# Three stages of a graph network kernel re-ordered: maxima scanned a block ahead, tables split by two engines, and some one-hot halves built by ScalarE

## The reference

```python
Q = relu(x @ query_kernel + query_bias)[row]        # 8 heads of 16
K = relu(x @ key_kernel + key_bias)[col]
V = (x @ kernel)[col]
att = sum(Qh * Kh, axis=-1)                          # scores, one per edge and head
smax = segment_max(att, row); sexp = exp(att - smax[row])
alpha = sexp / segment_sum(sexp, row)[row]
out = segment_sum(Vh * alpha, row) + bias
x = layernorm(x + out)        # then L1 (edge MLP with batch norms), L2 (graph convolution), L3 (GIN with MLP)
```

## Time and profile before

| | us |
|---|---|
| median of 3 runs | 11621.56 (11620.08 to 11631.48) |
| the profiled execution, its own time | 11608.96 |
| its span in the profile | 11607.3 |
| DVE busy in the span | 8568.2 (74%) |
| PE busy in the span | 8888.0 (77%) |
| ACT busy in the span | 4243.8 (37%) |

### The profile page before, as it was taken

How to read it: one execution, slowest core, us unless ns; L and a number is a source line. 1 busy time by engine, 2 the same in 40 slices (tenths; PEclk the granted TensorE clock), 3 DMA queues, 4 the chain that set the end, 5 groups by cost and what they waited for, 6 DMA issues and landing times. The chain is left out here.

```text
span 11607.3 us, 329950 instructions
## 1 busy us (share of the span) xinstructions
PE 8888.0 (77%) x100902; PEld 7202.7 (62%) x101099; DVE 8568.2 (74%) x17497; ACT 4243.8 (37%) x8562; POOL 1651.7 (14%) x2115
## 2 busy tenths in 40 slices
PE   6144557885888744799994888799899959949996
PEld 5132224664777644799994666433899946649995
DVE  7497777777999856666666666666788877788887
ACT  0020001111333211455552333477677736613332
POOL 0010000110000000466661000000000003301110
PEclk5555555555999855899997999899999979979997
DMA  1100000000444311233331999687455510000000
GB/s 37 13 0 11 4 4 8 11 11 21 162 160 162 125 33 32 96 122 124 123 124 67 328 324 327 234 251 250 129 144 144 144 41 5 5 3 3 3 3 12
DMA packets 616505, 1103.16 MB, mean 95 GB/s; under 512 B 119451, under 2 KB 207094, under 8 KB 616443
## 3 DMA queue, kind: packets, MB, share of 16 engines
q1 hardware_dynamic: 486939, 922.77, 25.0%
q10 hardware_dynamic: 121152, 168.86, 3.9%
q0 software_dynamic: 8352, 10.85, 0.4%
HBM read 901.13 MB, written 201.10 MB: 95 GB/s over the span
## 5 line engine op out<-in xcount | busy, mean ns | idle before, releaser
L2364 POOL TENSOR_TENSOR acc<-acc,m_sum 128x544 f32<-128x544 f32 (+1 forms) x637 | 809.8, 1271 | 1289.7 <-ACT m_sum L2331 1012.8
L2294 PE MATMUL m_sps<-m_msg,m_oh 128*128 128x136 f32 x5096 | 722.8, 286 | 0.0
L2229 DVE TENSOR_TENSOR m_msg<-m_vps,m_msg 128x512 f32<-128x512 f32 x637 | 440.5, 692 | 367.0 <-PE m_vps L2270 292.2
L2684 PE MATMUL u_sps<-u_r,u_oh 128*128 128x128 f32 x5096 | 677.8, 276 | 28.7 <-ACT u_r L2642 28.7
L2483 DVE BATCH_NORM_STATS2 stats<-t_es 128x512 f32 x637 | 442.3, 694 | 331.0 <-ACT t_es L2516 329.3
L2668 PE MATMUL u_zps<-fcs,u_a 128*128 128x128 f32 x5112 | 676.9, 276 | 6.9 <-ACT u_a L2636 6.9
L1983 ACT COPY s_qs<-s_qps 128x512 f32<-128x512 f32 x637 | 372.9, 585 | 800.9 <-PE s_qps L1964 727.8
L1397 PE MATMUL sp_out_x<-x,sp_adj_x 128*128 128x128 f32 x4802 | 661.9, 281 | 0.0
L1964 PE MATMUL s_qps<-q_parts,s_oht 128*128 128x128 bf16 x7203 | 511.5, 220 | 194.0 <-DVE s_oht L1461 168.2
L2569 PE MATMUL g_z<-g_a,fcT 128*128 128x512 f32 x1274 | 611.5, 615 | 62.9 <-ACT g_a L2558 52.8
L1381 PE MATMUL sp_aps_x<-sp_ohw_x,sp_oh_x 128*128 128x128 bf16 x7644 | 545.8, 219 | 144.7 <-DVE sp_ohw_x L1348 144.7
(11 more groups left out here) (582 smaller groups left out, 21327.1 us busy)
## 6 DMA issues: line engine op xcount, KB each, us to landing
u_e<-e_tiles SPq DMA_DIRECT2D x640, 256.0 KB, 2.8
e_tiles<-t_es ACTq DMA_DIRECT2D x637, 256.0 KB, 5.3
g_e<-e_tiles SPq DMA_DIRECT2D x637, 256.0 KB, 3.4
s_rows<-bucket_rows SPq DMA_DIRECT2D x148, 768.0 KB, 4.1
m_rows<-bucket_rows SPq DMA_DIRECT2D x148, 768.0 KB, 4.1
t_rows<-bucket_rows SPq DMA_DIRECT2D x148, 768.0 KB, 6.8
s_rows<-bucket_rows SPq DMA_DIRECT2D x49, 1024.0 KB, 5.3
m_rows<-bucket_rows SPq DMA_DIRECT2D x49, 1024.0 KB, 5.3
```

Source lines behind the costliest of these rows:

```text
L2294: last = nc.tensor.matmul(sps[x][:, at:at + M], oh[x][:, j * P:(j + 1) * P], msg[x][:, j * M:(j + 1) * M], start=True, stop=True)
L2364: nc.gpsimd.tensor_tensor(at, at, sums[x][:, 0:n * M], ALU.add).then_inc(added, 1)
L2684: last = nc.tensor.matmul(sps[:, :], oh[x][:, j * P:(j + 1) * P], zr[x][:, j * D:(j + 1) * D], start=(q == 0 and j == 0), stop=(q == last_ ...
```

## The change

Three edits.

1. `phase_parts`: the table is cut into two halves `u` of 25 blocks. DVE keeps the four half subtractions and two half casts; ACT does the other four half casts. Four more semaphores are taken.
2. `phase_scores`: for the sets 3, 5, 7, 9 and 11 (`shared`) DVE builds only the left 512 columns. ACT builds the right 512 by two instructions: the square of (row number - node number), and then relu(1 - that), which is 1 where they are equal and else 0. The square stands ahead of ACT's copy of set `q = p - 2`, the relu behind it. PE waits for ACT's half too, and DVE, before it frees a piece, waits for ACT's sets of that piece.
3. `phase_maxima`: the turning of `x_att` and the scan of window `w + 1` are issued within window `w`. Window 0's stand ahead of the loop, and SP loads one window more behind its loop. The three block numbers of the spare tiles are packed into one integer, so that one register load and shifts take the place of three register loads.

```diff
+    def overs(self, eng, s, b):
+        packed = eng.value_load(self.ovpk[0:1, bass.ds(b, 1)], min_val=0, max_val=64 ** self.OV - 1)
+        return [((packed >> 6 * j) & 63).with_bounds(min_val=0, max_val=s.NB) for j in range(self.OV)]
...
@@ phase_parts
+        at = [slice(0, s.NB1 // 2), slice(s.NB1 // 2, s.NB1)]
+        def cast(copy, u, c):
+            return copy(p4[:, at[u], c, :], blocks(rest if c else src)[:, at[u], :]).then_inc(made[u], 1)
             @block.vector
-                c.step(nc.vector.tensor_copy(p4[:, :, 0, :], blocks(src)))
-                c.step(nc.vector.tensor_tensor(blocks(rest), blocks(src), p4[:, :, 0, :], ALU.subtract))
-                c.step(nc.vector.tensor_copy(p4[:, :, 1, :], blocks(rest)))
-                c.step(nc.vector.tensor_tensor(blocks(rest), blocks(rest), p4[:, :, 1, :], ALU.subtract))
-                c.step(nc.vector.tensor_copy(p4[:, :, 2, :], blocks(rest)))
+                def lessen(u, c):
+                    dve.wait_ge(made[u], c + 1)
+                    nc.vector.tensor_tensor(blocks(rest)[:, at[u], :], blocks(rest if c else src)[:, at[u], :], p4[:, at[u], c, :],
+                                            ALU.subtract).then_inc(less[u], 1)
+                cast(nc.vector.tensor_copy, 0, 0)
+                lessen(0, 0)
+                lessen(1, 0)
+                lessen(0, 1)
+                lessen(1, 1)
+                dve.wait_ge(less[1], 2)
+                cast(nc.vector.tensor_copy, 1, 2)
...
+            @block.scalar
+                cast(nc.scalar.copy, 1, 0)
+                for u, c in ((0, 1), (1, 1), (0, 2)):
+                    act.wait_ge(less[u], c)
+                    cast(nc.scalar.copy, u, c)
...
@@ phase_scores
+        shared = range(3, NQ - 1, 2)
...
-                    row_hots(nc, k, B, oht[r], buf[n], q).then_inc(oht_made[r], 1)
+                    if q in shared:
+                        nc.vector.tensor_scalar(oht[r][:, 0:GE], row_of(0, q), k["iota1_p"][:, 0:1], None, ALU.is_equal).then_inc(oht_made[r], 1)
+                    else:
+                        row_hots(nc, k, B, oht[r], buf[n], q).then_inc(oht_made[r], 1)
                     if q + 1 == B.pieces[n][1]:
                         dve.wait_ge(oht_made[r], O.before(w, q) + 1)
+                        here = [p for p in shared if p < B.pieces[n][1]]
+                        if here:
+                            dve.wait_ge(act_made, w * len(shared) + (len(here) + 1))
                         dve.sem_inc(rows_free[n], 1)
...
                     for q in range(NQ):
                         x = X.slot(q)
+                        p, n = q + 2, w * len(shared)
+                        if p in shared:
+                            back, user = O.user_before(p)
+                            act.wait_ge(rows_in[piece_of(B, p)], w * 16 + 16)
+                            act.wait_ge(k_made[X.slot(user)], X.before(w, user) + (1 + k0 + back * X.uses[X.slot(user)]))
+                            act.wait_ge(act_made, n + (shared.index(p) + 1))
+                            nc.scalar.activation(far[:, :], row_of(1, p), ACT.Square, bias=minus[:, 0:1]).then_inc(far_made, 1)
                         act.wait_ge(q_made[x], X.before(w, q) + 1)
                         act.wait_ge(prod_made[x], X.before(w, q) + 1)
                         nc.scalar.copy(qs[x][:, :], qps[x][:, :]).then_inc(q_copied[x], 1)
+                        if p in shared:
+                            act.wait_ge(far_made, n + shared.index(p) + 1)
+                            nc.scalar.activation(oht[O.slot(p)][:, GE:], far[:, :], ACT.Relu, bias=1.0, scale=-1.0).then_inc(act_made, 1)
...
@@ phase_maxima, vector
-                    dve.wait_ge(turned, w + 2)
-                    dve.wait_ge(back, w + 1)
-                    nc.vector.tensor_tensor_scan(run[:, :], mask[:, bass.ds(half * GE, GE)], tps[0:HQ, :], 0.0, ALU.mult, ALU.max).then_inc(scanned, 1)
                     hot(0)
                     hot(1)
                     b = B.block(dve, s, w)
-                    vs = [dve.value_load(B.ovsb[0:1, bass.ds(b * OV + j, 1)], min_val=0, max_val=s.NB) for j in range(OV)]
+                    vs = B.overs(dve, s, b)
                     hot(2)
                     hot(3)
                     dve.wait_ge(split, w * 5 + 2)
                     nc.vector.tensor_tensor(rest[:, :], bps[:, :], parts[0][:, :], ALU.subtract).then_inc(split, 1)
+                    scan(w + 1)
                     dve.wait_ge(split, w * 5 + 4)
                     nc.vector.tensor_tensor(rest[:, :], rest[:, :], parts[1][:, :], ALU.subtract).then_inc(split, 1)
```

More of the change, by code:

```diff
@@ L1094, in _ @@
                 c.go(nc.vector.tensor_copy(B.ovsb[:, :].rearrange("p (b q) -> p b q", q=OV), v4[0:1, :, F:]))
+                c.step(nc.vector.tensor_copy(pk[:, :], v4[0:1, :, F + OV - 1]))
+                for q in range(OV - 2, -1, -1):
+                    c.step(nc.vector.tensor_scalar(pk[:, :], pk[:, :], 64.0, None, ALU.mult))
+                    c.step(nc.vector.tensor_tensor(pk[:, :], pk[:, :], v4[0:1, :, F + q], ALU.add))
+                c.go(nc.vector.tensor_copy(B.ovpk[:, :], pk[:, :]))
                 c.step(nc.vector.tensor_copy(xc[:, :], xk))
@@ L1741, in phase_parts @@
         step, stored = sem("parts_step"), sem("parts_stored")
+        made, less = ([sem(f"parts_{x}{u}") for u in range(2)] for x in ("made", "less"))
         p4 = parts[:, :].rearrange("p (b c f) -> p b c f", c=3, f=D)
+        at = [slice(0, s.NB1 // 2), slice(s.NB1 // 2, s.NB1)]
+        def cast(copy, u, c):
+            return copy(p4[:, at[u], c, :], blocks(rest if c else src)[:, at[u], :]).then_inc(made[u], 1)
         with nc.Block() as block:
@@ L2006, in _, with load @@
             def _(sp):
-                with sp.Fori(0, B.windows(sp, s)) as w:
-                    half = w & 1
-                    sp.wait_ge(turned, w + 1)
-                    sp.wait_ge(free, w + 1)
+                nw = B.windows(sp, s)
+                def load(n, w):
+                    half = n & 1
+                    sp.wait_ge(turned, n + 1)
+                    sp.wait_ge(free, n + 1)
                     sp.sem_inc(go, 1)
@@ L2017, in _ @@
                                  ).then_inc(ins, 16)
-                    sp.wait_ge(ins, w * 32 + 32)
+                    sp.wait_ge(ins, n * 32 + 32)
                     sp.sem_inc(go, 1)
+                with sp.Fori(0, nw) as w:
+                    load(w, w)
+                load(nw, 0)
+                sp.wait_ge(att_in, nw * 32 + 32)
+                sp.sem_inc(go, 1)
             @block.tensor
@@ L2025, in _, with turn @@
                 pe.sem_inc(split, 1)
-                with pe.Fori(0, B.windows(pe, s)) as w:
+                def turn(w):
                     pe.wait_ge(att_in, w * 32 + 32)
@@ L2031, in _ @@
                     last.then_inc(turned, 1)
+                turn(0)
+                with pe.Fori(0, B.windows(pe, s)) as w:
                     pe.wait_ge(scanned, w + 2)
@@ L2036, in _ @@
                     last.then_inc(back, 1)
+                    turn(w + 1)
                     pe.wait_ge(split, w * 5 + 6)
@@ L2056, in _, with scan @@
                 r_last, S = R.slot(NQ - 1), s.NB * H
+                def scan(w):
+                    half = w & 1
+                    dve.wait_ge(ins, w * 32 + 32)
+                    dve.wait_ge(turned, w + 2)
+                    dve.wait_ge(back, w + 1)
+                    nc.vector.tensor_tensor_scan(run[:, :], mask[:, half * GE:(half + 1) * GE] if isinstance(w, int) else mask[:, bass.ds(half * GE, GE)],
+                                                 tps[0:HQ, :], 0.0, ALU.mult, ALU.max).then_inc(scanned, 1)
+                scan(0)
                 with dve.Fori(0, B.windows(dve, s)) as w:
                     half = w & 1
-                    dve.wait_ge(ins, w * 32 + 32)
                     def hot(q):
```

20 lines of the change are left out of this document (17 added, 3 removed).

## The result

| | before | after |
|---|---|---|
| median, us | 11620.93 (4 runs, 11620.08 to 11631.48) | 11549.77 (4 runs, 11540.65 to 11562.99) |
| ratio | | 0.9938, 95% interval 0.9926 to 0.9951 |
| the profiled execution's own time, us | 11608.96 | 11562.99 |

The change makes the kernel 71 us faster. The forecast was 104 us faster (11517); 11550 lies inside its range of 11485 to 11555, 33 us above its middle.

A forecast was written before the change was run, and what follows sets the result against it. No engine bounds the whole kernel; stages run one behind another, each edit acting on its own. 37 + 24 + 43 = 104 us off 11621.6 gives about 11517 us, 8 in 10 within 11485 to 11555.

The forecast's parts named there:

- Splits: forecast 37: Splits: six calls save 6.25 us each, ACT's casts being covered by DVE's work; 37 us, bounds 33 and 41.
- 2 x 3.49/2: Splits: DVE's two half casts take half of 3.49 us each, part of 17.15 us a call.
- The bound of 33: Splits: the lower bound of the gain, 33 us, with each handover costing 0.3.
- Scores: forecast 24: Scores: half one-hots save 0.60 us a window, less queue instructions; net 0.48, 24 us in 49 windows, bounds 0 and 46.
- 3 x 0.08 = 0.24 if all is exposed, and about half of it if the queue prepared it: Scores: cost per window, in us, of one queue instruction more for DVE at each of three piece ends.
- rival (b): Scores give nothing, because ACT's square pushes the copy or a half's pitch equals the whole's: 11541 us; chance 13%.
- rival (d): Scores: ACT reloads its function table between copy, square and relu, losing 314 us: slower, 11830 us; chance 2%.
- Maxima: forecast 43: Maxima: the cycle falls from 13.12 to 12.25 us, 0.87 less in 49 windows; 43 us, bounds 28 and 60.
- H + 5.9: Maxima: DVE's own route reaches the scan 5.9 us after H, the end of a window's one-hots.
- H + 6.0: Maxima: SP's mask load lets the scan start 6.0 us after the end of a window's one-hots, as late as DVE.
- rival (a): Maxima: the mask decides, taking over 5 us from issue to use; cycle 13.1, no gain there, 11560 us; chance 9%.
- rival (c): Maxima: PE's clock rises from 0.50, scatter falls from 4.30 to 3.1 us, 59 us more gain: 11458 us; chance 5%.

The follow-up runs named there:

- e2_scores_only: The kernel before with the `phase_scores` edit alone: 11606.39 us, ratio 0.9990 (0.9981 to 0.9999).
- e7_loads_late: The changed kernel with the window's block and the packed load read behind the second subtraction: 11534.99 us, ratio 0.9918 (0.9900 to 0.9937).
- e6_packed_only: The kernel before with the packed load and nothing else of the maxima edit: 11588.33 us, ratio 0.9977 (0.9966 to 0.9989).
- e5_ahead_three_loads: The changed kernel with three register loads again in place of the packed one: 11595.54 us, ratio 0.9977 (0.9967 to 0.9987).

## Why the prediction was right and wrong

**That each edit is worth what it does to its own stage** held for the change, whose three stages are that sum, and the direction, faster, held with it. It did not hold for the edits alone: the splits alone and the scores alone each made the maxima, a stage that they do not touch and that a barrier parts from them, 11 us longer.

**Splits: forecast 37, measured 20.** The step that failed is the term "2 x 3.49/2" for DVE's half casts, which the earlier trace rows seemed to give. Half the columns did not take half the time, since 50 blocks were cut into 25 and 25. Measured it is 2 x 3.49, 3.5 us a call more; the fixed costs that I had put at 0.1 each were nearly nil (six instructions in 20.75 us against 17.15 + 3.5), so a call saved 3.4 and not 6.2. Even halves gave 3.3 of it back. The bound of 33 had no place for it: it took a price as proportional without asking what speed the instruction ran at. The rest of this step was right: ACT's casts (2.86 for my 2.9) lie under DVE's subtractions. The Trainium skill has the rule that I passed over: "VectorE: DVE Perf Modes", section "What auto-detection actually checks", says that a one-source instruction runs two elements a cycle in f32 if source and destination are in SBUF and their outermost non-unit dimensions are both even or equal. The traces agree with it: 25 blocks on the strided side 3486 ns, 24 and 26 blocks 1762 and 1894. That the source's blocks collapse into one dimension, so that the two sides were not equal, is my reading of it; no run here tells that part alone.

**Scores: forecast 24, measured 17.5.** The mechanism was right and one size off. The half one-hots gave somewhat more than the 0.60 us a window that I had worked out: their pitch is 0.26 for 0.40 (means of 48 windows), and with SP waiting in DVE's place the stage fell by 32.9 us, 0.67 a window. The term "3 x 0.08 = 0.24 if all is exposed, and about half of it if the queue prepared it" was too small: I had taken 0.12 of it in the sum, and without it the change's stage gained 0.31 a window. The difference of 0.19 is 9 us in 49 windows, of which some 3 came back by the shorter one-hots. In `e2_scores_only` the same instructions cost 0.21, and the stage came to 22.4, close to the forecast; so some 5 us of the 6.5 that are missing hang on the one end of a piece at set 8, whose price differs between two kernels with the same source there. It was not lateness of ACT (0.7 us in all), as I had said, though DVE's idle ahead of the reduction at set 5, 0.37, passed the 0.35 that I had named as a sign. No product waited for ACT's copy, so rival (b) fell; rival (d) fell with the missing table loads.

**Maxima: forecast 43, measured 39, and for the most part for the reason given.** The packed load was put at 1.5 us for two loads, measured 1.43 (2.45 to 1.02). "Shifts at the end of the window cost some 0.2" was too small. Before, the large update and the three small ones stood so:

```profile
4317.70 0.56 DVE L2083 TENSOR_TENSOR most<-most,x_mps 128x392 f32<-128x392 f32 x1 [0.63 <-PE x_mps L2045]
...
4318.41 0.77 DVE L2086 TENSOR_TENSOR most<-most,x_mps 128x8 f32 x3
```

The last small one (0.16 long) started 1.32 us behind the large one; now it is 1.80 (4268.71 to 4270.51), 0.48 more. The 0.2 that the moved waits were to give back at the head came to 0.05 (idle of 0.58, now 0.53). So DVE came to the scan at H + 6.08 where I had H + 5.9; the 0.08 above the 6.0 that I took makes the missing 4 us. `e7_loads_late` showed the mask at H + 5.88 behind it, where I had H + 6.0. So rival (a) had the right next limit and did not decide here, by 0.2 us; it did as soon as DVE came earlier. The clock stayed at 0.50, which ends rival (c) (11458).

What the forecast did not see is that the scan ahead gave none of this gain: `e6_packed_only` has all of it without. With four loads (`e5_ahead_three_loads`) the scan ahead brings the one-hots 2 forward by 0.31 us (5.83 behind H, 6.14 before), and it costs 0.42 between the first subtraction and the scatter (3.01 us, before 2.59), where now the scan stands in place of a wait for ACT. Its worth, 1.1 to 1.4 us, appears only when loads and mask are off its path.

**Sum.** 104 against 77 by stages and 71 by medians: 17 of the missing 27 are the splits, 6 the scores, 4 the maxima. The range held it, but for a reason (17 us in the splits) that none of the bounds had: the room at its upper end was there for a late mask. In that it was luck.

**What stays open.** Why DVE's queue needs 0.81 in place of 0.58 us over the loop's head when the splits or the scores alone are changed; two instructions more did not reproduce it, and it was not tried with other counts. Whether the end of a piece at set 8 (0.93 or 0.83 us) has the same cause. What the scan ahead is worth beside splits and scores with the packed load in its place: its loop has 0.53 at the head in every kernel, so it may save there some 0.25 us a window that `e6_packed_only` can't show. And which part of the 30 us scatter of the `t_eps` stage hangs on the kernel: in one profiled execution each it was shortest for before (1022), which the medians do not bear out as an effect of the change.

## What to carry to other kernels

Halve a DVE instruction only after asking whether its speed stays. The cast from f32 to bf16 of a blocked table did not at an odd count of blocks, where the half cost as much as the whole, and did at even counts; the subtraction of the same halves did not care. A wait or a register load in a queue showed no price where its engine still had work or waited for another anyway, and 0.1 to 0.2 us (a wait) or 0.7 us (a load) where the engine had nothing else queued up, so put it on the engine that idles, or behind the last work that others wait for. Where two routes end within 0.2 us of each other, clear both in one edit: here the register loads alone gave 0.3 us a window beyond the change, the mask behind them 0.8 more. And time a stage whose source is untouched as well: here one moved by 0.23 us a window, 11 us, half of what the splits or the scores had gained.

## What the runs showed of the hardware that I had not expected

- A cast of 128x3200 f32 to bf16 as 25 blocks took DVE 3486 ns, as 24 or 26 blocks (3072 or 3328 columns) 1762 or 1894.
- A register load of 0.30 us costs DVE about 0.7 us with the queue instructions around it (idle of 2.45 us behind four loads, 1.02 behind two).
- The same queue instructions took DVE 0.58 or 0.81 us at the head of one loop, and 0.09 or 0.19 us at the end of one piece, in kernels that differ elsewhere.
- The granted clock can differ where nothing else does. The stretch 1050 to 1800, before (first) and after (second), code and durations alike:

```profile
1050.00:1800.00 750.00, 445.68 (x1689) 176.80 (x1689) 547.55 (x1293) 16.84 (x45) 0.00 (x0) 0.50 0.01 4
```

```profile
1050.00:1800.00 750.00, 445.27 (x1689) 176.21 (x1687) 545.73 (x1289) 16.92 (x45) 0.00 (x0) 1.00 0.01 4
```

  The matmuls there had a median of 420 ns in both, and the loop that they belong to took 818.0 and 818.6 us, so in this stage a granted clock of 1.2 or 2.4 GHz changed nothing that can be read from the rows, and the mean clock of the whole execution (0.816 before, 0.934 after) is no sign of a gain. Of the 43 executions of the kernel before that were timed beside the experiments, 19 had a mean clock over 0.93, with a median of 11622 us, and 18 one of 0.82 or less, with 11624 us.
- ACT's square and relu on 512 columns took 722 and 632 ns and ran between copies without a table load.
